# Wider operand splits, and small scale and count work moved from VectorE to ScalarE, in a 16-batch expert-and-pooling kernel

## The reference

```python
# layer 0, per batch
h      = gelu(x @ fc1_w.T + fc1_b)              # 2048 hidden
shared = h @ fc2_w.T + fc2_b                    # 384 outputs
expert = h @ experts_w[idx].T + experts_b[idx]  # 128 outputs, one of 16 experts
x      = x + concat(shared, expert)
# layer 1, per batch
scores = tanh(x @ W1 + b1) @ v                  # one score a token
mask   = prefix, postfix or all-but-self, by the batch's type
p      = softmax(where(mask, scores, -1e30))
x      = x + (p @ x) / count(mask)
```

## Time and profile before

| | |
|---|---|
| median of 3 runs | 1318.46 us (1318.44 to 1318.58) |
| span of the profiled execution | 1316.9 us |
| its own time beside the span | not given apart; the median is 1.6 us above the span |
| TensorE busy with matmuls | 1309.4 us, 99% |
| TensorE weight loads | 906.2 us, 69% |
| VectorE busy | 1117.0 us, 85% |
| ScalarE busy | 953.3 us, 72% |
| GpSimd busy | 117.4 us, 9% |

### The profile page before, as it was taken

How to read it: one execution, slowest core, us unless ns; L and a number is a source line. 1 busy time by engine, 2 the same in 40 slices (tenths; PEclk the granted TensorE clock), 3 DMA queues, 4 the chain that set the end, 5 groups by cost and what they waited for, 6 DMA issues and landing times.

```text
span 1316.9 us, 24025 instructions
## 1 busy us (share of the span) xinstructions
PE 1309.4 (99%) x9261; PEld 906.2 (69%) x9261; DVE 1117.0 (85%) x2132; ACT 953.3 (72%) x1716; POOL 117.4 (9%) x220
## 2 busy tenths in 40 slices
PE   9999999999999999999999999999999999999998
PEld 5458476585867858577685866858678585876855
DVE  7998998778979798787988979789797987879898
ACT  5868958588685877858679586886858678586762
POOL 0000000020100101011020100201001010100102
PEclk9999999999999999999999999999999999999999
DMA  8410011021010201002110110110102010120006
GB/s 300 145 57 32 1 65 33 16 74 32 34 42 33 65 33 41 25 33 65 32 50 17 41 57 33 57 40 26 41 33 65 33 43 23 33 81 1 35 19 120
DMA packets 30678, 66.07 MB, mean 50 GB/s; under 512 B 6227, under 2 KB 7651, under 8 KB 28131
## 3 DMA queue, kind: packets, MB, share of 16 engines
q1 hardware_dynamic: 28834, 61.65, 14.3%
q0 software_dynamic: 1152, 2.09, 1.2%
q10 hardware_dynamic: 576, 0.79, 0.2%
HBM read 45.65 MB, written 18.87 MB: 49 GB/s over the span
## 4 chain that ended last, share of the span: by engine, by line
PE 97%; DVE 2%; issue 0%; ACT 0%; DVEq 0%
PE ps L482 14%; PE ps L483 14%; PE ps L484 14%; PE ps L567 10%; PE ps L568 10%; PE ps L569 10%; PE ps L578 6%; PE ps L586 5%; PE ps L587 5%; DVE hh L1597 1%; DVE hl L1597 1%; PE ps L464 1%; PE ps L468 1%; PE ps L466 1%; PE ps L453 1%; PE ps L647 1%
## 5 line engine op out<-in xcount | busy, mean ns | idle before, releaser
L484 PE MATMUL ps<-xh,w1l 128*128 128x256 f16 x960 | 261.7, 273 | 0.0
L482 PE MATMUL ps<-xh,w1h 128*128 128x256 f16 x960 | 261.7, 273 | 0.0
L483 PE MATMUL ps<-xl,w1h 128*128 128x256 f16 x960 | 261.7, 273 | 0.0
L931 ACT ACTIVATE g<-ps,b1s,ds 128x512 f32<-128x512 f32 x240 | 173.6, 773 | 71.6 <-PE ps L484 71.6
L482 PE MATMUL ps<-xh,ch 128*128 128x256 f16 x720 | 196.4, 273 | 0.0
L483 PE MATMUL ps<-xl,ch 128*128 128x256 f16 x720 | 196.2, 273 | 0.0
L484 PE MATMUL ps<-xh,cl 128*128 128x256 f16 x720 | 196.2, 273 | 0.0
L1493 DVE SCALAR_TENSOR_TENSOR hl<-g,ix,hh 128x512 f16<-128x512 f32 x243 | 178.1, 746 | 3.0
L906 ACT ACTIVATE hh<-g,ix 128x512 f16<-128x512 f32 x243 | 161.5, 717 | 0.0
L569 PE MATMUL ps<-hl,w2h 128*128 128x512 f16 x384 | 145.5, 379 | 0.0
L567 PE MATMUL ps<-hh,w2l 128*128 128x512 f16 x384 | 145.5, 379 | 0.0
(11 more groups left out here) (345 smaller groups left out, 2855.2 us busy)
## 6 DMA issues: line engine op xcount, KB each, us to landing
space<-in_xT SPq DMA_DIRECT2D x62, 256.0 KB, 3.1
er<-in_ew SPq DMA_DIRECT2D x15, 1024.0 KB, 4.9
out<-space SPq DMA_DIRECT2D x60, 256.0 KB, 2.3
space<-in_w SPq DMA_DIRECT2D x29, 256.0 KB, 6.0
er<-in_w SPq DMA_DIRECT2D x3, 1024.0 KB, 9.4
out<-sums POOLq DMA_DIRECT2D x8, 255.5 KB, 4.8
space<-in_ew SPq DMA_DIRECT2D x1, 1024.0 KB, 6.0
out<-xn SPq DMA_DIRECT2D x3, 256.0 KB, 3.0
```

The lines of the kernel that those rows point to most:

```text
L482: mm(to, wh, mh, start=i in (1, 5) and c == 0, stop=False, skip_group_check=True)
L483: mm(to, wh, ml, start=False, stop=False, skip_group_check=True)
L484: m = mm(to, wl, mh, start=False, stop=c == 1, skip_group_check=True)
L931: act(in_two(g_of(b, k)), src, ACT.Gelu, bias=b1s[:, k:k + 1], scale=ds1[:, b % 2, p:p + 1]).then_inc(gelu_done)
```

## The change

- x is split in four calls: X11 with X21, T1 with T2 and T3 with T4 in calls of 1024 columns, X22 alone. T4's high part is therefore made with T3's, ahead of the evacuations of ROW and ROW2; before, it came after `first_of_sum`.
- The expert's weights of batches 1 to 15 are split in two calls of 1024 columns in place of four of 512.
- ds1, ds2 and is2 of the next batch are made by ScalarE (`output_scales`, five calls, ahead of the split of X11), not by VectorE.
- The token counts of `one_way` are made by ScalarE, after its exponentials.
- The four totals of `one_way` are one call; its steps are reordered (34 in place of 38), and `turn` runs in cycles 4 to 7.
- In the correction products all eight matmuls with the high part of h come first, then the eight with the low part; `sum6` waits for the sum on hh before the first eight, and for the sum on hl only before the second.

```diff
@@ -204,7 +204,8 @@
 
     X11, X21, X22, T1, T2, T3, T4 = range(7)
     MOVING = {1: X11, 2: X21, 3: X22, 4: T4, 5: T1, 6: T2, 7: T3}
-    X_ORDER = (X11, T1, T2, X21, T3, X22, T4)
+    X_ORDER = (X11, T1, T3, X22)
+    GROUP = {X11: X11, X21: X11, T1: T1, T2: T1, T3: T3, T4: T3, X22: X22}
     W1_ORDER = (3, 4, 5, 6, 7, 0, 8, 9, 1, 10, 11, 12, 13, 14, 15, 2)
     W1_LOW_ORDER = (3, 4, 5, 6, 7, 0, 1, 8, 9, 10, 11, 12, 13, 14, 15, 2)
     eye = er[:, 0, 2 * S:2 * S + P]
@@ -268,11 +269,16 @@
     def combined(t):
         return in_two(g[:, t - T1, :])
 
-    def operand(b, t):
-        return {X11: (0, 0), X21: (1, 0), X22: (1, 1)}[t] if t < T1 else None
-
-    def x_part(b, t):
-        return quarter(b, *operand(b, t)) if t < T1 else combined(t)
+    def x_group(b, t):
+
+        if t == X11:
+            return xr[:, b % XB, :, LEFT]
+        return quarter(b, 1, 1) if t == X22 else g[:, t - T1:t - T1 + 2, :]
+
+    def split_group(parts, t):
+        if t == X11:
+            return parts[:, X11:X21 + 1, :].rearrange("p a (c n) -> p (a c) n", n=HALF)
+        return in_two(parts[:, X22, :]) if t == X22 else parts[:, t:t + 2, :]
 
     def either_way(b, c, turned):
         s = b % XB + 1
...
@@ -337,6 +346,20 @@
     def nth_tile(b, k):
         return NH * b + k + 1
 
+    def nth_expert(b, part):
+
+        return 2 * b + part + 3 if b else part + 1
+
+    def expert_whole(b):
+        return nth_expert(b, 1 if b else 3)
+
+    def expert_of_tile(b, k):
+        return nth_expert(b, k // (8 if b else 4))
+
+    def expert_part(b, t, part):
+        n = NH // (2 if b else 4)
+        return t[:, n * part:n * (part + 1)]
+
     def nth_pair(b, p):
         return PAIRS * (b - 1) + p + 1
 
...
@@ -355,7 +378,8 @@
     def nth_seed(b, o):
         return 4 * b + (o + 1 if b == 0 else (2, 1, 3, 4)[place_of(b, o)])
 
-    T3_HIGH, T2_DONE, T4_DONE, LEFT_DONE, T1_DONE, Y_ADDED, ROW_DONE, X_ADDED, ROW2_DONE, S_STEPS = 2, 4, 6, 7, 9, 10, 11, 12, 13, 13
+    T3_HIGH, T2_HIGH, T2_DONE, T4_DONE, LEFT_DONE, T1_DONE, Y_ADDED, ROW_DONE, X_ADDED, ROW2_DONE, S_STEPS = (
+        2, 3, 4, 6, 7, 9, 10, 11, 12, 13, 13)
     W_SUMS, W_SUMS_LOW = 7, 8
 
     def nth_product(b, i):
...
@@ -579,11 +603,13 @@
                 if k == NH - 1:
                     m.then_inc(fc2_done)
 
-        def products(i, to, first=False):
+        def products(i, to, first=False, low_ready=0):
 
             (wh, wl), (ks, n) = W_OF[i], H_OF[i]
             for k in range(HALF_K):
                 mm(to, wl[:, k, :], hh[:, ks.start + k, n], start=first and k == 0, stop=False, skip_group_check=True)
+            e.wait_ge(s_step, low_ready)
+            for k in range(HALF_K):
                 m = mm(to, wh[:, k, :], hl[:, ks.start + k, n], start=False, stop=k == HALF_K - 1, skip_group_check=True)
             m.then_inc(s_done)
 
...
@@ -598,8 +624,8 @@
 
         def sum6(b):
             e.wait_ge(s_copied, nth_copy(b, 1))
-            e.wait_ge(s_step, s_value(b, T2_DONE))
-            products(6, half_bank(SY, 0))
+            e.wait_ge(s_step, s_value(b, T2_HIGH))
+            products(6, half_bank(SY, 0), low_ready=s_value(b, T2_DONE))
 
         def sum7(b):
             e.wait_ge(s_copied, nth_copy(b, 2))
...
@@ -952,20 +978,20 @@
             e.wait_ge(ix_done, e_chain(b))
             if b:
                 e.wait_ge(fc2_done, 4 * b)
-            copy(flat(eh[:, 4 * q:4 * q + 4, :]), expert_rows(b)[:, 512 * q:512 * q + 512], scale_of(ec(b))).then_inc(eh_done)
+            copy(expert_part(b, eh, q), expert_part(b, expert_tiles(b), q), scale_of(ec(b))).then_inc(eh_done)
 
         def split_x_high(b, t):
             if t < T1:
                 for c in range(KD):
                     e.wait_ge(x_in[b % XB * KD + c], x_loaded(b))
             else:
-                e.wait_ge(combos, 4 * (b - 1) + t - T1 + 1)
+                e.wait_ge(combos, 4 * (b - 1) + t - T1 + 2)
             e.wait_ge(ix_done, x_chain(b))
             if b == 1:
                 e.wait_ge(tile_done, NH)
             else:
                 e.wait_ge(p3, nth_pair(b - 1, PAIRS - 1))
-            copy(in_two(xh[:, t, :]), x_part(b, t), scale_of(xc(b))).then_inc(xh_done)
+            copy(split_group(xh, t), x_group(b, t), scale_of(xc(b))).then_inc(xh_done)
 
         def squares(b, i, c, src):
             if b == 1:
...
@@ -1000,6 +1026,15 @@
             if nth_pair(b, p) > 2:
                 e.wait_ge(added1, nth_pair(b, p) - 2)
             copy(fifth[:, p % 2, :], half_bank(7, 0)).then_inc(fifth_copied)
+
+        def output_scales(b):
+
+            i, h = b % 2, slice(hc(b), hc(b) + 1)
+            e.wait_ge(ix_done, x_chain(b))
+            copy(ds1[:, i, :], ex[:, w1c:w1c + PAIRS], ex[:, xc(b):xc(b) + 1]).then_inc(ds1_done)
+            for lo, hi, col in ((3, 4, ec(b)), (0, 3, w2c)):
+                copy(ds2[:, i, lo:hi], ex[:, col:col + hi - lo], ex[:, h])
+                copy(is2[:, i, lo:hi], ix[:, col:col + hi - lo], ix[:, h]).then_inc(ds2_done)
 
         def seed(b, o):
 
...
@@ -1083,14 +1118,19 @@
             e.wait_ge(pool_step, pool_value(b, 9))
             act(cell(b, 19), cell(b, 19), ACT.Exp)
             act(weights_and_ratio, weights_and_ratio, ACT.Exp, bias=cell(b, 18)).then_inc(exp_done)
+            e.wait_ge(io_in, 16)
+            e.wait_ge(mask_step, TABLES)
+            if b > 1:
+                e.wait_ge(x_out[(b - 1) % XB * KD + 2], x_stored(b - 1))
+            act(count_of, io[:, :], ACT.Identity, bias=cnt_from[:, b:b + 1], scale=cnt_by[:, b:b + 1]).then_inc(inverted)
 
         def inverses(b):
 
-            e.wait_ge(pool_step, pool_value(b, 14))
+            e.wait_ge(pool_step, pool_value(b, 13))
             if b > 1:
                 e.wait_ge(x_out[(b - 1) % XB * KD + 3], x_stored(b - 1))
             act(inverse_of, mt, ACT.Ln, scale=sign[:, b:b + 1]).then_inc(inverted)
-            e.wait_ge(inverted, 2 * b - 1)
+            e.wait_ge(inverted, 3 * b - 1)
             act(inverse_of, inverse_of, ACT.Exp, scale=-1.0).then_inc(inverted)
             eng.preload_act_table(ACT.Gelu)
 
...
@@ -1142,7 +1182,6 @@
         def paired_opening(b):
             n = b + 1
             first_of_sum(b)
-            split_x_high(n, T4)
             second_of_sum(b)
             third_of_sum(b)
             fifth_copy_of_sum(b)
...
@@ -1247,12 +1286,10 @@
                     sums_high(c + 3)
             cycle(b, PAIRS)
             split_expert_high(b, 0)
-            split_expert_high(b, 1)
             gelu_pair(b, PAIRS - 1)
             high(b, NH - 2)
             high(b, NH - 1)
-            split_expert_high(b, 2)
-            split_expert_high(b, 3)
+            split_expert_high(b, 1)
             if b == LAST:
                 break
             e_squares(b + 1)
...
@@ -1267,10 +1304,10 @@
             if paired(b):
                 seed(b, ROW)
                 one_way_exponentials(b - 1)
-                for t in (X11, T1, T2):
-                    split_x_high(b + 1, t)
+                output_scales(b + 1)
+                split_x_high(b + 1, X11)
+                split_x_high(b + 1, T1)
                 split_x2_high(b, 0)
-                split_x_high(b + 1, X21)
                 evacuate(b, 3)
                 seed(b, ROW2)
                 inverses(b - 1)
...
@@ -1287,10 +1324,9 @@
             else:
                 exponentials(b - 1)
             split_x2_high(b, 0)
+            output_scales(b + 1)
             split_x_high(b + 1, X11)
             split_x_high(b + 1, T1)
-            split_x_high(b + 1, T2)
-            split_x_high(b + 1, X21)
             if scanned_once(b - 1):
                 inverses(b - 1)
             evacuate(b, 1)
...
@@ -1445,10 +1480,11 @@
 
         def batch_scales(b):
             chain_scale(8 + b, hc(b), hc(b) + 3 if b > 1 else NC)
-            fc1_scale(b, 8 + b, 0, PAIRS)
-            out_scales(b, 8 + b, 3, 4, ec(b))
-            out_scales(b, 8 + b, 0, 3, w2c)
+            e.wait_ge(ix_done, 8 + b)
             if b == 1:
+                fc1_scale(b, 8 + b, 0, PAIRS)
+                out_scales(b, 8 + b, 3, 4, ec(b))
+                out_scales(b, 8 + b, 0, 3, w2c)
                 e.wait_ge(ex_done, 9)
                 eng.tensor_reduce(x2_tmp[:, 1:2], ex[:, w2c:w2c + 3], AX.X, ALU.max).then_inc(vmax_done)
                 e.wait_ge(vmax_done, 6)
...
@@ -1506,13 +1542,13 @@
                      flat(w2h[:, o, 4 * q:4 * q + 4, :])).then_inc(w2l_done)
 
         def expert_low(b, q):
-            e.wait_ge(eh_done, nth_chunk(b, q))
-            low_part(flat(el[:, 4 * q:4 * q + 4, :]), expert_rows(b)[:, 512 * q:512 * q + 512], scale_of(ec(b)),
-                     flat(eh[:, 4 * q:4 * q + 4, :])).then_inc(el_done)
+            e.wait_ge(eh_done, nth_expert(b, q))
+            low_part(expert_part(b, el, q), expert_part(b, expert_tiles(b), q), scale_of(ec(b)),
+                     expert_part(b, eh, q)).then_inc(el_done)
 
         def x_low(b, t):
```

(122 more changed lines are left out.)

4 lines of the change are left out of this document (2 added, 2 removed).

## The result

| | before | after |
|---|---|---|
| median of 4 runs | 1318.52 us (1318.44 to 1318.71) | 1334.53 us (1334.24 to 1334.79) |
| span of the profiled execution | 1316.9 us | 1332.4 us |
| VectorE busy | 1117.0 us | 1086.3 us |
| ScalarE busy | 953.3 us | 960.2 us |

The ratio is 1.0121, with a 95% interval from 1.0109 to 1.0133: the change made the kernel 16.0 us slower. The direction was forecast; the size was 11.4 us, and 1334.53 lies just outside the range that ended at 1334. A term of 6.6 us was missing, one was 1.8 us too large and another 0.3.

The account below looks back on a forecast made before the run. The prediction took TensorE, with almost no idle time, to bound the kernel. Its terms, -2.6 + 2.0 + 12.0 = +11.4 us on the 1318.46 us median, gave 1329.9 us, range 1317.5 to 1334.

Parts of the forecast that it names:

- What bounds the kernel, and the ceiling of the gain: TensorE, busy 1309.4 of 1316.9 us, bounds the kernel; only its standstill can be saved, at most 2.6 us (0.20%).
- `sum6`'s gap: TensorE loses 0.22 us before sum6 waiting for the hl sum; it goes in 12 batches, -2.6 us.
- The expert's wider split: Before k = 14 of fc2(b, 0), low parts come 0.30 later against 0.17 us of cover: 15 x 0.13 = +2.0 us.
- ScalarE's stretch: ScalarE's work ahead of the first_of_sum copy grows 2.02 us, 1.01 absorbed: 1.0 us standstill before sum2, 12 batches, +12.0 us.
- The start: ScalarE's exponentials, released by step 9 of one_way behind low(b, 15) on VectorE's queue, begin 0.30 us later.
- the room of 0.88 us: Slack on ScalarE up to sum2: 0.17 before evacuate(b, 3), 0.59 idle, 0.09 overlap, 0.03 at sum2.
- Off the path: VectorE loses some 3 us of work a batch and stays ahead of TensorE where it matters: gives nothing.
- the two signs of being wrong: Small ScalarE calls starting every 0.1 us or less, or step 9 of one_way coming as early as before.
- The rivals: All waits vanish, 1315.8 us, chance 0.05; only the el wait costs, 1317.9, 0.15; small calls do not overlap, 1336.4, 0.10.
- the first: Rival: ScalarE's additions and the el half find room, so only the gain remains: 1315.8 us, chance 0.05.

Follow-up runs that it names:

- Experiment 2: Changed kernel with ds1, ds2 and is2 made by VectorE again, none by ScalarE: 1323.80 us, 10.7 less than the changed kernel.
- experiment 7: Changed kernel with ScalarE's five scale calls moved, in paired batches, behind the second copy of the block products: 1324.19 us, 10.3 less.
- 6: Kernel before with only the making of ds1, ds2 and is2 moved to ScalarE: 1320.13 us, 1.5 more, ratio 1.0011.
- Experiment 1: Changed kernel with one pooling step instead of two between add_fifth and add_row2, the scan taken after add_second: 1327.68 us, 6.9 less.
- experiment 5: Kernel before with three pooling steps instead of two between add_fifth and add_row2, the third a scan: 1327.31 us, 8.6 more, ratio 1.0066.
- experiment 8: Changed kernel with the scan's place, the scales on ScalarE and the expert's split in two calls undone together: 1315.20 us, ratio 0.9974.
- experiment 4: Kernel before with only the high-part correction products first and sum6 waiting for the hl sum before the second eight: 1315.76 us, ratio 0.9978.

## Why the prediction was wrong

**What bounds the kernel, and the ceiling of the gain.** Right. The 31 us that VectorE lost (2 us in each of 15 batches, where some 3 were forecast) gave nothing; the only gain was `sum6`'s gap, forecast as 2.6 us and measured alone as 1318.61 - 1315.76 = 2.85.

**The expert's wider split.** Right: 0.13 us in 15 batches was forecast, 0.11 found, 1.7 us instead of 2.0.

**ScalarE's stretch.** The mechanism and the prices were right, one input was not. The counts cost 0.70 (forecast 0.70) and the scales 0.94 (0.95). The start was 0.17 us later instead of 0.30. The step counted bounds, which stands ahead of the exponentials on VectorE's queue, as work alone, but bounds also waits for ScalarE's squares. In the kernel before it was the last square that ended its wait (706.77 + 0.19 = 706.96, bounds at 707.00, 0.70 us after the start of the last combine at 706.30); with the wide split the squares come earlier, and bounds starts 0.60 us after that combine (713.36, 713.96). So 0.10 us of VectorE's delay was taken up there. The hole is 0.85 us instead of 1.0, 10.2 us instead of 12.0. Experiment 2 gives 10.7 for it and the hole near 181 us, 7 shows that the place costs and not the work, and 6 that the stretch had about the room of 0.88 us that was counted (0.94 us more left `sum2`'s load 0.06 late).

**Off the path.** This is the step that failed. It said of VectorE that it "stays ahead of TensorE at the points that matter, so this gives nothing". I priced what the merged totals and the removed counts save, and followed the wait for x_low of T3, but not what the renumbering does to each `pool(n)`: with the total taken out of the pair between `add_fifth` and `add_row2`, the next step moves in, and that is a scan. A total and a product (0.27 and 0.68 by their rows) became a product and a scan (0.68 and 1.23), 1.05 us more ahead of `x2_low(b, ROW)`. The missing term is 12 x (0.33 + 0.22) = 6.6 us. Experiment 1 gives 6.9 when it is undone; experiment 5 makes it in the kernel before, 8.6 us for a hole that is 0.18 us larger, as there the total, which takes 0.18 us until the next call (656.44, 656.62), is still ahead of it.

**The sum.** -2.6 + 1.7 + 10.2 + 6.6 = 15.9 us against 16.0 measured. The three terms that were forecast, at the sizes found, give 1318.5 + 9.3 = 1327.8 us, and experiment 1, which lacks only the fourth, took 1327.68. The range, which had its upper end from ScalarE's prices alone, left no room for a step not looked at, and the two signs of being wrong that the prediction named (small calls 0.1 us apart, step 9 as early as before) did not come: they too looked only at ScalarE.

**The rivals.** None of the three came. The Trainium skill's rule on grouping ("Perfetto Trace Analysis", "Optimizing Scalar/DVE Operations"), which stood beside the first, speaks of a saturated engine; VectorE was busy for 85% of the span and ScalarE for 72%. The wide splits of x are still in experiment 8, which is faster than the kernel before by 0.26%; the reordered products alone give 0.22% (experiment 4), and the intervals overlap, so no run here shows a gain from the wide splits.

## What to carry to other kernels

In a kernel like this one, whose matmul engine has next to no idle time, an edit on the other engines is worth nothing until it touches a wait, and then its price is what exceeds the room there: the same five calls cost 1.5 us or 10.7, by what else stood in the stretch, and nothing that shows where ScalarE was idle (experiment 7). So count the room of every hand-over to the matmul engine first (idle time ahead of it, plus slack behind it), and then go through every slot of the queue that the edit renumbers. Where steps are dealt out by count, a step removed early changes which step stands in each later slot; write out the list of what each slot holds before and after, with durations, even where the total gets less.
